# Where ACT's normalization stands in a window-attention and blur kernel, and in which step its readers run

## The chip, the cores and the metric

The program runs on one core of a Trainium2 chip. The metric is the device time of one execution in microseconds (us), lower is better. The engines are PE (TensorE), DVE (VectorE), ACT (ScalarE), POOL (GpSimd) and SP (SyncE), which here does nothing but issue DMAs. PEld are PE's weight loads.

## The reference

For each of 32 images of 192 channels and 56x56 pixels, in float32:

```python
x = x + attention(gn(x))      # gn: group norm, 32 groups
x = x + blur(gn(x))

# attention: 8x8 windows of 7x7 pixels, 12 heads of 16 channels
qkv = einsum('bchw,oc->bohw', x, w_qkv)
dots = einsum('wnid,wnjd->wnij', q, k) * scale + bias[None]
out = einsum('wnij,wnjd->wnid', softmax(dots), v)
out = einsum('bchw,oc->bohw', out, w_proj) + b_proj
# blur: channels shifted by whole pixels and filtered by 5x5 Gaussian taps
```

## The kernel before, in words

The image is the unit of an outer loop, and its 64 windows are taken as 32 pairs. One turn of `for p in range(PAIRS)` is called a **step** here; an image has steps 0 to 31, and every engine has its own written-out list of what it does in step p. `bodies` runs the image loop on each engine. Each body works on three images at once: `prev` (i-1, its second norm and blur), `att` (i, attention), `nxt` (i+1, its first norm). The order on an engine is that of the source; semaphores (`S[...]`) alone tie engines together. SP's DMAs stand in such a list too, and SP issues them strictly one after another.

What a pair p goes through:

- `scores` (PE, in step p-1), `maximum` (DVE), `turn` (PE, the transpose at L604, once a step), `shift_hi` (ACT, `mov`, L832) and `shift_lo` (DVE), `shifted` (PE, L613 and L620).
- In step p+1 `exp` (ACT, L827), `prob_hi` (DVE, L1045), `prob_lo` (POOL, L1201).
- In step p+2 `attend` (PE, L637, first thing in the step), `normalize` (DVE, `osb`). In p+3 `out_hi` (ACT, L840), `out_lo` (POOL, L1207), `turn_out` (PE, L647), `turned_out` (ACT, `om`, L848, last thing in ACT's step). `attend` of the next step waits for `turned_out`, since both share the bank `pO`.

What runs beside it, by tables of step numbers:

- `norm_step`: four steps for each chunk of two rows of windows. `norm` (ACT, L784) writes the normalized tokens twice, in float32 (`xnf`) and in float16 (`xnh`, of the last 64 channels `xnt`); `norm_lo` (POOL) and `tail_lo` (DVE, L993) form the low half from the two one step later.
- `qk_step`: query and key projections in steps 6 to 11, 14 to 19, 22 to 27 and 30 to 3 (`qk`, PE, L505 to L550 into `pQ`; `qk_hi`, ACT; `qk_lo`, DVE). The first of each four waits for all four `tail_lo` and `norm_lo` of its chunk.
- `v_step`: `values` (PE, into `pV`) in odd steps, `LEAD` = 5 pairs ahead, then `v_hi`, `v_lo`.
- `proj_step`: the output projection of window row r (`project`, PE, L658, into `pV`) in step 4r+6 (128 channels) and 4r+8 (the last 64), then `project_out` (ACT) and `add_residual` (POOL). It waits for the last `turned_out` of its row, which ACT does in that same step 4r+6.
- `blur_step`: stages of one image's blur in 16 steps each, PE's from step 13.
- SP: `stack` copies heads for `scores` (36 DMAs for each chunk), `spread_v` copies values (4 DMAs, L431), `store_x1` (L440, L442), `read_x1` (one DMA of 2.35 MB into `xr`, L448), the loads of the next image (L480, L482), the stores of the output (L492).

Of the kernel before, what the change touches and what calls it, by code (L numbers as in the profile page):

```python
# [34 lines left out]
C, HW = 192, 56  # L35
# [34 lines left out]
LEAD = 5  # L70
# [67 lines left out]
def build(nc, x, w_in, b_out, table, rel, offset, cf, ch, scratch, out):  # L138
    images = x.shape[0]
    ctx = ExitStack()  # L140
    with ctx:
# [93 lines left out]
        PER = {"x_in0": 16, "x_in": 48, "x1_out": 256, "xr_in": 16, "y_out": 8 * 16, "stack_q": 192 * NCH,  # L235
# [64 lines left out]
        def v_step(p, att, nxt):  # L300

            if p % 2 and (att if p + LEAD < PAIRS else nxt):
# [75 lines left out]
        def _(sp):  # L378
# [67 lines left out]
            def read_x1():  # L446

                sp.dma_start(xr[0:SY, :], scratch.rearrange("s y c x -> (s y) (c x)")).then_inc(S["xr_in"], 16)  # L448

            def body(i, prev, att, nxt):  # L450
                for p in range(PAIRS):
                    v = before(v_step, p, prev, att, nxt) if p % PPR == 2 else None
# [7 lines left out]
                    if p == 4 and prev:  # L460
                        store_x1(i - 1, NCH - 1)
                    if p == 5 and prev:
# [4 lines left out]
                        read_x1()  # L467
                    if p in (2, 6) and nxt:
# [12 lines left out]
                        for h in (0, 1) if p == 6 else ():  # L481
                            sp.dma_start(xt[64 * h:64 * h + 64, par(i + 1), :],  # L482
                                         xi[CM:C, h * (TOK // 2):(h + 1) * (TOK // 2)]).then_inc(S["x_in"], 16)
                    b = blur_step(p, 15, prev)
# [17 lines left out]
        def _(pe):  # L502
# [180 lines left out]

            def body(i, prev, att, nxt):
                for p in range(PAIRS):
# [7 lines left out]
                    b = blur_step(p, 13, prev)  # L693
# [15 lines left out]
                    v = v_step(p, att, nxt)  # L709
                    for n, row, tail in was:  # L710

                        if v and tail_bank(row if tail else 0) is pV:
                            pe.wait_ge(S["pj_act"], nth("pj_act", i + n, 2 * row + tail + 1))
                    if v:
# [16 lines left out]
                    if prev and p == 5:  # L731
# [4 lines left out]
                    if prev and p == 6:  # L736
                        pe.wait_ge(S["gn2_dve"], nth("gn2_dve", i - 1, 6))
                        group_sum(2, pM, gv[1]).then_inc(S["gn2_pe"], 1)
                    if prev and p == 9:
# [13 lines left out]
        def _(act):  # L753
# [6 lines left out]
            def norm(i, c, s):  # L760

                row, tail = 2 * c + s % 2, s // 2
                act.wait_ge(S["gn1_pool"], nth("gn1_pool", i, 2))

                done = PPC // 2 * (c - 1) - (0 if s % 2 else 2)
# [515 lines left out]
```

## Time and profile before

| | |
|---|---|
| Times of three executions | 6164.22, 6182.63 (median), 6187.85 us |
| The profiled execution's own time | 6163.97 us |
| Its span on the core | 6162.2 us |
| PE, DVE, ACT, POOL busy, share of the span | 88%, 69%, 62%, 58% |
| Granted clock of PE, mean share of 2.4 GHz | 0.929 |
| DMA engines busy, mean of 16 | 55% |

### The profile page before, as it was taken

What the parts mean: (1) busy time and instruction counts of PE and PEld (TensorE: products, weight loads), DVE (VectorE), ACT (ScalarE), POOL (GpSimd) and SP (SyncE); (2) the same over time, 40 slices, a digit from 0 to 9 for tenths busy, and PEclk for the clock granted to TensorE, in tenths of its full rate; (3) what the DMA queues carried; (4) which work ended last, traced back from release to release, by engine and by line L of the source; (5) the groups of instructions that cost most, each with busy time, mean ns of one, the idle gap of its engine ahead of it and who ended that gap; (6) DMA issues with size and microseconds to landing.
All of it is one profiled execution on the core that took longest, in us unless ns stands there. A gap on an engine that the chain in (4) does not pass through costs nothing. (4 is left out here: it accounts for less than half of the span.)

```text
span 6162.2 us, 258882 instructions
## 1 busy us (share of the span) xinstructions
PE 5409.0 (88%) x97992; PEld 4490.2 (73%) x97992; DVE 4255.1 (69%) x9682; ACT 3790.8 (62%) x8451; POOL 3580.1 (58%) x3940
## 2 busy tenths in 40 slices
PE   5888889988898888889888898888898889899896
PEld 3777777777777777777777777777777777777775
DVE  3776667777777767777767777767777766677763
ACT  1666666666666666666666666666666666666662
POOL 0565556665556655566655566655566655566654
PEclk9999999999999999999999999999999998999996
DMA  2555655555655555655555655555655555555553
GB/s 61 123 130 138 138 134 120 129 134 136 139 134 117 135 135 132 141 132 118 137 134 133 143 127 122 137 133 136 137 128 127 134 137 134 134 123 127 133 118 72
DMA packets 1352972, 790.32 MB, mean 128 GB/s; under 512 B 1187528, under 2 KB 1237128, under 8 KB 1344008
## 3 DMA queue, kind: packets, MB, share of 16 engines
q1 hardware_dynamic: 1351816, 774.03, 55.1%
q8 instruction: 832, 13.63, 1.0%
q14 instruction: 324, 2.65, 0.1%
HBM read 157.09 MB, written 154.14 MB: 51 GB/s over the span
## 5 line engine op out<-in xcount | busy, mean ns | idle before, releaser
L1207 POOL TENSOR_TENSOR o<-osb,o 128x192 f16<-128x192 f32 x1024 | 624.5, 610 | 1768.8 <-ACT o L840 1754.1
L1201 POOL TENSOR_TENSOR probl<-prob,probh 98x588 f16<-98x588 f32 x1024 | 1332.5, 1301 | 298.1 <-DVE probh L1045 183.8
L637 PE MATMUL pO<-vv,probh 98*49 98x34 f16 x24576 | 1023.2, 225 | 103.9 <-ACT om L848 85.6
L637 PEld LDWEIGHTS pO<-vv,probh 98*49 98x49 f16 x24576 | 872.6, 122 | 313.1 <-issue 251.7
L832 ACT ACTIVATE mov<-pT 12x98 f16<-12x98 f32 x1024 | 248.1, 242 | 1329.6 <-PE pT L604 1329.5
L637 PE MATMUL pO<-vv,probl 98*49 98x34 f16 x12288 | 995.2, 228 | 54.5 <-issue 54.5
L637 PEld LDWEIGHTS pO<-vv,probl 98*49 98x49 f16 x12288 | 778.0, 122 | 58.4 <-issue 58.3
L1030 DVE TENSOR_REDUCE mx<-pS 128x12 f32<-128x588 f32 x1024 | 777.2, 759 | 34.1 <-issue 15.9
L620 PE MATMUL pT<-qst,kst 96*98 96x49 f16 x12288 | 760.4, 208 | 11.5 <-issue 11.4
L827 ACT ACTIVATE prob<-pT 98x588 f32<-98x588 f32 x1024 | 672.3, 657 | 105.8 <-PE pT L620 97.2
L620 PEld LDWEIGHTS pT<-qst,kst 96*98 96x98 f16 x12288 | 696.5, 133 | 13.8 <-issue 13.6
L1045 DVE CAST probh<-prob 98x588 f16<-98x588 f32 x1024 | 531.4, 519 | 203.9 <-ACT prob L827 191.0
L586 PE MATMUL pS<-biasT,addb 128*64 128x294 f16 x4096 | 619.2, 312 | 18.4 <-DMA kst<-mix 17.3
L594 PEld LDWEIGHTS pS<-kst,qst 96*64 96x64 f16 x12288 | 589.2, 118 | 30.0
L594 PE MATMUL pS<-kst,qst 96*64 96x98 f16 x12288 | 610.9, 214 | 0.0
L1050 DVE RECIPROCAL rden<-pO 128x12 f32<-128x12 f32 x1024 | 233.3, 228 | 521.2 <-PE pO L637 516.4
L613 PE MATMUL pT<-mov,biasT 128*98 128x98 f16 x6144 | 479.0, 218 | 32.0 <-DVE mov L1036 29.0
L1036 DVE SCALAR_TENSOR_TENSOR mov<-pT,mov 12x98 f16<-12x98 f32 x1024 | 257.4, 251 | 354.0 <-ACT mov L832 338.7
L1004 DVE SCALAR_TENSOR_TENSOR mix<-pQ,cst,mix 128x392 f16<-128x392 f32 (+1 forms) x512 | 320.8, 627 | 242.7 <-ACT mix L810 239.0
L1231 POOL TENSOR_TENSOR xc<-xcf,xc 114x336 f16<-114x336 f32 x512 | 447.4, 874 | 69.3 <-ACT xc L891 30.2
L613 PEld LDWEIGHTS pT<-mov,biasT 128*98 128x98 f16 x6144 | 398.5, 133 | 73.4 <-ACT mov L832 45.3
L1242 POOL TENSOR_TENSOR xcf<-xr,coef 114x336 f32<-114x336 f32 x512 | 384.6, 751 | 105.7 <-DVE coef L1123 57.0
(190 smaller groups left out, 16140.3 us busy)
## 6 DMA issues: line engine op xcount, KB each, us to landing
kst<-kh SPq DMA_DIRECT2D x1536, 98.0 KB, 2.2
qst<-qh SPq DMA_DIRECT2D x1536, 49.0 KB, 2.3
qst<-mix SPq DMA_DIRECT2D x768, 98.0 KB, 2.9
kst<-mix SPq DMA_DIRECT2D x768, 98.0 KB, 2.2
vv<-cv SPq DMA_DIRECT2D x1024, 73.5 KB
xr<-x_scratch SPq DMA_DIRECT2D x32, 2352.0 KB, 12.3
out<-xr SPq DMA_DIRECT2D x256, 294.0 KB
x_scratch<-xm SPq DMA_DIRECT2D x256, 196.0 KB, 3.3
```

The costliest lines, as they stand in the source:

```text
L586: pe.matmul(pS[half, bank, 0:HB], addb[:, half], biasT[:, HB * bank:HB * bank + HB], start=True, stop=False, skip_group_check=True)
L594: mm = pe.matmul(o, qst[:, c % 2, t:t + 64], kst[:, c % 2, hp, PW * w:PW * w + PW], start=False, stop=True, skip_group_check=True)
L613: pe.matmul(pT[0:98, bank, at:at + PW], biasT[:, PW * hp:PW * hp + PW], mov[:, :], start=(hp % 3 == 0), stop=False, skip_group_check=True)
L620: mm = pe.matmul(pT[0:98, bank, a:a + NT], kst[:, c % 2, hp, PW * w:PW * w + PW], qst[:, c % 2, t:t + NT], start=False, stop=True, skip_gr ...
L637: mm = pe.matmul(pO[64 * win:64 * win + NT, OW * hp:OW * hp + OW], b[0:98, p % 2, PW * hp + NT * win:PW * hp + NT * win + NT], vv[:, g % 2 ...
L827: act.activation(banked(prob[0:98, p % 2, :]), pT[0:98, :, 0:HB], ACT.Exp).then_inc(S["exp_a"], 1)
L1030: dve.tensor_reduce(mx[:, :].rearrange("p (b h) -> p b h", b=2), src, AX.X, ALU.max).then_inc(S["max_d"], 1)
L1045: dve.tensor_copy(probh[0:98, p % 2, :], prob[0:98, p % 2, :]).then_inc(S["ph_d"], 1)
L1201: pool.tensor_tensor(probl[0:98, p % 2, :], prob[0:98, p % 2, :], probh[0:98, p % 2, :], ALU.subtract).then_inc(S["pl_p"], 1)
L1207: pool.tensor_tensor(o16[:, p % 2, C:2 * C], osb[:, p % 2, :], o16[:, p % 2, 0:C], ALU.subtract).then_inc(S["ol_p"], 1)
L1231: pool.tensor_tensor(xc[:, b % 2, 1, :], xcf[0:SX, b % 2, :], xc[:, b % 2, 0, :], ALU.subtract).then_inc(S["xcl_p"], 1)
L1242: pool.tensor_tensor(v, src, spread(coef[:, cols], HW), ALU.mult).then_inc(S["xcf_p"], 1)
```

## The change

1. `norm_step` gives every norm one step earlier (1, 9, 17, 25 in place of 2, 10, 18, 26).
2. On ACT `norm` is called twice in a step, for one output each: the float32 one ahead of `shift_hi`, with the waits, and the float16 one at the step's end, behind `turned_out`. The number of instructions stays.
3. `LEAD` is 6 and `values` run in even steps; in steps with neither `qk` nor blur they are issued ahead of `turn_out` and `shifted` on PE. Projections move to odd steps: 4r+7 and 4r+9, and 4r+8 for the tail of the last row.
4. Blur and the second norm move one step later. `read_x1` becomes two DMAs of half the size, in SP's steps 6 and 8; the second part of the next image's load moves from step 6 to 7.

```diff
-LEAD = 5
+LEAD = 6
...
-            for lo, shift, c, on in ((2, 0, 2, att), (10, 0, 3, att), (18, 1, 0, nxt), (26, 1, 1, nxt)):
+            for lo, shift, c, on in ((1, 0, 2, att), (9, 0, 3, att), (17, 1, 0, nxt), (25, 1, 1, nxt)):
...
-            if p % 2 and (att if p + LEAD < PAIRS else nxt):
+            if p % 2 == 0 and (att if p + LEAD < PAIRS else nxt):
...
-                    s = PPR * r + 6 + (LATE_TAIL if tail and r < NWX - 1 else 0)
+                    s = PPR * r + 7 + (0 if not tail else LATE_TAIL if r < NWX - 1 else 1)
...
-            def read_x1():
-
-                sp.dma_start(xr[0:SY, :], scratch.rearrange("s y c x -> (s y) (c x)")).then_inc(S["xr_in"], 16)
+            def read_x1(s):
+
+                sp.dma_start(xr[HW * s:HW * s + HW, :],
+                             scratch[s].rearrange("y c x -> y (c x)")).then_inc(S["xr_in"], 16)
...
-                    v = before(v_step, p, prev, att, nxt) if p % PPR == 2 else None
+                    v = before(v_step, p, prev, att, nxt) if p % PPR == 1 else None
...
-                    if p == 4 and prev:
+                    if p == 5 and prev:
                         store_x1(i - 1, NCH - 1)
-                    if p == 5 and prev:
+                    if p == 6 and prev:
...
-                        read_x1()
-                    if p in (2, 6) and nxt:
+                        read_x1(0)
+                    if p == 8 and prev:
+                        read_x1(1)
+                    if p in (2, 7) and nxt:
...
+                    v = v_step(p, att, nxt)
+                    early = v and not q and b is None
+                    if early:
+                        given_back(i, was)
+                        values(i + v[0], v[1])
...
-                for o in (full, hi):
-                    a = act.activation(wmajor(o), src, ACT.Identity, bias=gbias[g, tail:tail + 1],
-                                       scale=grs[0][g, tail:tail + 1])
-                a.then_inc(S["xnh_a"], 1)
+                    o = xnh[:, t] if hi else xnf[:, s % 2, :]
+                a = act.activation(wmajor(o), src, ACT.Identity, bias=gbias[g, tail:tail + 1],
+                                   scale=grs[0][g, tail:tail + 1])
+                if hi:
+                    a.then_inc(S["xnh_a"], 1)
...
+                    n, q = norm_step(p, att, nxt), qk_step(p, att, nxt)
+                    if n:
+                        norm(i + n[0], n[1], n[2], False)
                     if att:
                         shift_hi(i, p)
...
-                    n = norm_step(p, att, nxt)
-                    if n:
-                        norm(i + n[0], n[1], n[2])
-                    q = qk_step(p, att, nxt)
                     if q:
                         qk_hi(i + q[0], q[1], q[2])
-                    for n, q in at(p, 3, prev, att, nxt):
-                        turned_out(i + n, q)
+                    for m, o in at(p, 3, prev, att, nxt):
+                        turned_out(i + m, o)
+                    if n:
+                        norm(i + n[0], n[1], n[2], True)
...
-                            pool.wait_ge(S["xr_in"], nth("xr_in", i - 1, 16))
+                            pool.wait_ge(S["xr_in"], nth("xr_in", i - 1, 32))
```

ACT in the image loop, from one `mov` (`shift_hi`) to the next `prob` (`exp`), in step 2. Before:

```order
L832 ACTIVATE mov<-pT 12x98
L763 ISA
L767 REGISTER_ALU
L769 REGISTER_ALU
L774 ISA
L784 ISA
L784 ACTIVATE xnf<-xm,gbias,grs 128x392
L784 ACTIVATE xnh<-xm,gbias,grs 128x392
L789 REGISTER_ALU
L807 ACTIVATE mix<-pQ,cst 128x8x49
L810 ACTIVATE mix<-pQ,cst 64x8x49
L848 ACTIVATE om<-pO 128x3x98
```

The same place now (`xnf` ahead of `mov`, `xnh` behind `om`):

```order
L793 ACTIVATE xnf<-xm,gbias,grs 128x392
L840 REGISTER_ALU
L842 ACTIVATE mov<-pT 12x98
L799 REGISTER_ALU
L817 ACTIVATE mix<-pQ,cst 128x8x49
L820 ACTIVATE mix<-pQ,cst 64x8x49
L858 ACTIVATE om<-pO 128x3x98
L793 ACTIVATE xnh<-xm,gbias,grs 128x392
L837 ACTIVATE prob<-pT 98x588
```

The copy `om` has moved ahead of one normalization of its step, and the other now stands in front of `mov`.

SP in the image loop, from the last store of the previous image to the key stack of chunk 2. Before:

```order
L442 DMA x_scratch<-xt 32x14x56
L448 DMA xr<-x_scratch 112x5376
L425 REGISTER_ALU
L431 DMA vv<-cv 49x8x96 x4
L480 ISA
L480 DMA xm<-in_x 128x784
L482 ISA
L482 DMA xt<-in_x 64x1568
L482 ISA
L482 DMA xt<-in_x 64x1568
L407 REGISTER_ALU
L413 DMA qst<-qh 32x784 x12
```

And now:

```order
L442 DMA x_scratch<-xt 32x14x56
L448 DMA xr<-x_scratch 56x5376
L483 ISA
L483 DMA xm<-in_x 128x784
L485 ISA
L485 DMA xt<-in_x 64x1568
L485 ISA
L485 DMA xt<-in_x 64x1568
L407 REGISTER_ALU
L413 DMA qst<-qh 32x784 x12
L448 DMA xr<-x_scratch 56x5376
L425 REGISTER_ALU
```

The values' copies `vv` have moved ahead of the store, and the second half of the read stands behind the twelve `qst` copies.

## Rows read from the trace of the kernel before

**Rows 1.** The page: busy time by engine; the granted clock in 40 slices

```profile
PE 5409.0 (88%) x97992; PEld 4490.2 (73%) x97992; DVE 4255.1 (69%) x9682; ACT 3790.8 (62%) x8451; POOL 3580.1 (58%) x3940
...
PEclk9999999999999999999999999999999998999996
```

**Rows 2.** Waits of PE: who waited for whom, us, times, longest

```profile
PE pV L658 <- ACT om L848: 194.4, 125, 1.8
PE pQ L505 <- DVE xnt L993: 146.3, 128, 7.4
PE pO L637 <- ACT om L848: 85.6, 141, 1.2
PE pO L637 <- issue: 56.7, 27, 3.5
...
PE pS L586 <- DMA kst<-mix: 17.3, 11, 4.5
```

**Rows 3.** Timeline of ACT and PE, step 2 of image 12: start, duration

```profile
2361.07 0.75 ACT L784 ACTIVATE xnf<-xm,gbias,grs 128x392 f32 x1 [0.23 <-issue]
...
2361.72 0.73 ACT L784 ACTIVATE xnh<-xm,gbias,grs 128x392 f16 x1
...
2363.55 0.41 ACT L848 ACTIVATE om<-pO 128x294 f16<-128x294 f16 x1
...
2364.11 0.33 PE L658 MATMUL pV<-om,wmh 128*128 128x392 f16 x1 [1.76 <-ACT om L848]
```

**Rows 4.** Timeline of DVE and PE, step 6 of the same image

```profile
2385.17 0.55 DVE L993 TENSOR_TENSOR xnt<-xnf,xnt 64x392 f16<-64x392 f32 x1
...
2385.86 0.49 PE L505 MATMUL pQ<-xnh,wmh 128*128 128x392 f16 x1 [1.18 <-DVE xnt L993]
```

**Rows 5.** Stretches: steps 7, 16 and 5; length, engines busy, clock, DMA

```profile
2392.29:2396.64 4.35, 4.35 (x94) 3.77 (x91) 3.91 (x11) 2.38 (x6) 1.81 (x4) 1.00 1.10 297
2444.68:2449.97 5.29, 5.29 (x106) 4.32 (x102) 4.89 (x11) 3.81 (x9) 3.84 (x5) 1.00 0.27 66
2377.64:2384.41 6.77, 6.21 (x97) 5.74 (x93) 3.59 (x9) 3.43 (x7) 3.15 (x3) 0.75 0.95 287
```

**Rows 6.** Waits of ACT; then ACT's group of one normalization form

```profile
ACT mov L832 <- PE pT L604: 1329.5, 1023, 7.6
...
L784 ACT ACTIVATE xnf<-xm,gbias,grs 128x392 f32 x240 | 178.9, 745 | 7.7 <-issue 7.0
```

**Rows 7.** Timeline of PE: the first transpose of image 2 and of image 30

```profile
485.57 0.27 PE L604 MATMUL pT<-cst,mx 128*12 128x128 f32 x1
...
5700.73 0.27 PE L604 MATMUL pT<-cst,mx 128*12 128x128 f32 x1
```

**Rows 8.** Waits of SP's DMA queue

```profile
SPq L431 <- DVE cv L1022: 335.1, 110, 8.8
SPq L448 <- DMA x_scratch<-xt: 92.3, 32, 3.8
```

**Rows 9.** Timeline of SP in image 12: DMA issues, merged, duration of the issuing

```profile
2387.79 0.59 SPq L442 DMA_DIRECT2D x_scratch<-xt  x1
2391.40 0.35 SPq L448 DMA_DIRECT2D xr<-x_scratch  x1
2391.88 10.65 SPq L431 DMA_DIRECT2D vv<-cv  x4
...
2413.57 3.34 SPq L431 DMA_DIRECT2D vv<-cv  x4
...
2442.64 8.48 SPq L413 DMA_DIRECT2D qst<-qh  x12
2456.71 4.12 SPq L431 DMA_DIRECT2D vv<-cv  x4
```

**Rows 10.** DMA issues: KB each, us to landing

```profile
xr<-x_scratch SPq DMA_DIRECT2D x32, 2352.0 KB, 12.3
```

**Rows 11.** Timeline of POOL, step 10: the first use of `xr`

```profile
2411.37 0.75 POOL L1242 TENSOR_TENSOR xcf<-xr,coef 114x336 f32<-114x336 f32 x1 [1.02 <-DVE coef L1123]
```

More of the change, by code:

```diff
@@ L682, in blur, with given_back @@
                 mm.then_inc(S["c1_pe" if stage == 0 else "c2_pe"], 1)
+            def given_back(i, was):
+                for n, row, tail in was:
+                    if tail_bank(row if tail else 0) is pV:
+                        pe.wait_ge(S["pj_act"], nth("pj_act", i + n, 2 * row + tail + 1))
             def body(i, prev, att, nxt):
@@ L692, in body @@
                         turn(i, p)
-                    b = blur_step(p, 13, prev)
+                    b = blur_step(p, 14, prev)
                     if b is not None:
@@ L708, in body @@
                         blur(i - 1, b, 1)
[L709 to L714, printed above, removed]
+                    if v and not early:
+                        given_back(i, was)
                         values(i + v[0], v[1])
@@ L758, in _, with norm @@
             act.wait_ge(S["setup"], SET_ALL)
-            def norm(i, c, s):
+            def norm(i, c, s, hi):
                 row, tail = 2 * c + s % 2, s // 2
-                act.wait_ge(S["gn1_pool"], nth("gn1_pool", i, 2))
-                done = PPC // 2 * (c - 1) - (0 if s % 2 else 2)
-                if due("v_pe", i, done):
-                    act.wait_ge(S["v_pe"], nth("v_pe", i, done))
-                if due("qk_pe", i, 6 * (c - 1)):
-                    act.wait_ge(S["qk_pe"], nth("qk_pe", i, 6 * (c - 1)))
-                if tail:
-                    act.wait_ge(S["xnl_p"], nth("xnl_p", i, 2 * c + s - 1))
-                elif due("xtl_d", i, 2 * c + s - 1):
-                    act.wait_ge(S["xtl_d"], nth("xtl_d", i, 2 * c + s - 1))
+                if not hi:
+                    act.wait_ge(S["gn1_pool"], nth("gn1_pool", i, 2))
+                    done = PPC // 2 * (c - 1) - (0 if s % 2 else 2)
+                    if due("v_pe", i, done):
+                        act.wait_ge(S["v_pe"], nth("v_pe", i, done))
+                    if due("qk_pe", i, 6 * (c - 1)):
+                        act.wait_ge(S["qk_pe"], nth("qk_pe", i, 6 * (c - 1)))
+                    if tail:
+                        act.wait_ge(S["xnl_p"], nth("xnl_p", i, 2 * c + s - 1))
+                    elif due("xtl_d", i, 2 * c + s - 1):
+                        act.wait_ge(S["xtl_d"], nth("xtl_d", i, 2 * c + s - 1))
                 t = slice(ROW * (row % 4), ROW * (row % 4) + ROW)
@@ L1092, in body @@
                         maximum(i, p)
-                    if prev and p == 5:
+                    if prev and p == 6:
                         aggregate(1, i - 1)
@@ L1140, in body @@
                                      ).then_inc(S["gn2_bn"], 1)
-                    for n, t, on in ((0, 0, att and p == 26), (0, 1, att and p == 30), (-1, 2, prev and p == 2),
-                                     (-1, 3, prev and p == 4)):
+                    for n, t, on in ((0, 0, att and p == 27), (0, 1, att and p == 31), (-1, 2, prev and p == 3),
+                                     (-1, 3, prev and p == 5)):
                         if on:
```

41 lines of the change are left out of this document (20 added, 21 removed).

## The prediction

> **What bounds the kernel now.** Read first the busy shares and the granted clock [rows 1]: PE is busy 88% of the span and nothing else is over 69%, and the clock falls a little in most slices. So PE is the engine whose gaps cost time. Next the waits of PE [rows 2]. Three of them are large, and all three lead to ACT's step: the projection waits for `om` (194.4 us), the query projection for `xnt` (146.3), `attend` for `om` (85.6). Together 426.3 us, over 32 images 13.3 us an image. Then the timeline of one such place [rows 3]: in step 2 ACT does both normalizations (0.75 and 0.73 us) and a key copy before `om`, which starts at 2363.55; PE starts projecting at 2364.11 after 1.76 us of nothing. Step 6 shows the other kind [rows 4]: the last `xnt` is written in the step in which PE needs it, 1.18 us idle.
>
> Then ask which other resource is close behind. SP has no busy share, so take its waits [rows 8]: 335.1 us for the values' low halves and 92.3 us for its own stores, 427.4 us in all, 13.4 us an image. All other time it issues. An image takes (5700.73 - 485.57) / 28 = 186.3 us [rows 7], so SP works 186.3 - 13.4 = 172.9 us of it. That twelve copies cost it 8.48 us, 0.71 each, is seen in [rows 9]. PE already waits 11 times for a stack that SP brought late (17.3 us [rows 2]). SP is the second limit, and a near one.
>
> PE alone would allow much less: a step with a query and a value projection and no wait takes 4.35 us, one with blur 5.29 [rows 5]. Sixteen of each are 154 us; with the group sums and the steps that lack filler I put PE's own floor at 160.
>
> **Part by part.**
>
> *Norm one step earlier.* The last `tail_lo` of a chunk falls in step 5, 13, 21, 29, the query projection that needs it in 6, 14, 22, 30. `tail_lo` takes 0.55 us [rows 4], so a whole step of slack covers it: the 146.3 us go (4.6 an image). What ACT's norm waits for (the readers of the buffer it overwrites) lies further back, since `values` are also one step earlier.
>
> *Projections one step later.* In 4r+7 the row's last `om` is a step old. The 194.4 us go (6.1 an image). The residual and the second norm's statistics come later with them, which is why blur moves by a step too: its distance to them shrinks for the last row alone, whose tail is now two steps later while blur is one.
>
> *Norm in two parts.* The number of instructions stays, so this adds nothing to ACT's busy time. The first part (0.745 us [rows 6]) stands ahead of `mov`, where ACT waits 1329.5 us in 1023 cases, 1.30 us on average [rows 6]; that idle time hides it. `om` comes earlier by both parts in its step, so `attend` need not wait for it: 85.6 us go (2.7 an image). The second part stands ahead of `exp`; `exp` feeds DVE and POOL and is needed by `attend` two steps on, more than a step of slack. If the cover in front of `mov` is gone, `mov` is late, and with it PE's `shifted`: step 16, with keys and blur and without norm, has ACT busy 3.81 us of 5.29 [rows 5]; with the two parts (0.75 + 0.73 [rows 3]) that is 5.29, just PE's time. Six steps an image are so full. I charge nothing for them beside SP, and at most 0.3 us each, which is in the range.
>
> *Values in even steps, and early where PE has no filler.* The same matmuls. The order on SP changes: `spread_v` is a step earlier, so SP finds its data sooner. I price it with SP.
>
> *The read in two halves.* The whole read (2.35 MB, 12.3 us to landing [rows 10]) blocks SP: the four value copies behind it take 10.65 us where others take 3.34 [rows 9], 7.3 us too many. Halves of about 6 us, with other issues between them, should block less. It can go from 0 (the same bytes, and the loads of the next image now stand right behind the first half) to all 7.3. I take a third, 2.3 us, nearer to the lower end, because the bytes are the same. PE's own "issue" wait of 56.7 us [rows 2] lies in the window of that read; I credit nothing, because PE is no longer the limit.
>
> **The sum.** PE's side gives 186.3 - 13.3 = 173.0 at today's clock. SP's side gives 172.9 of work, plus 2.9 for its own stores (92.3 / 32; nothing stands between the stores and the read, so it stays), minus 2.3 of blocking, plus what is left of the waits for values. These are 10.5 an image now (335.1 / 32), between 0 and 10.5 after. I take 1.5, near zero, because a PE that runs 6% faster asks SP for the same copies in less time, so SP is late more often than early. 172.9 + 2.9 - 2.3 + 1.5 = 175.0 us. The two sides are close; SP's is the larger one, and the time follows it. Saved are 11.3 us in each of 31 images (the first has no blur beside it): 350 us. The profiled execution took 6163.97 us, its span being 6162.2, so 5814. It is the fastest of those shown; scaled to their median (6182.63 / 6163.97 = 1.003) this is 5831, and I say 5830.
>
> The clock: step 5 runs at 0.75 and takes 6.77 us [rows 5], and the mean is 0.929. Fewer PE waits should raise it, but where SP sets the pace a faster PE only waits longer, so it has no term of its own.
>
> What the Trainium skill says of SP's cost ("DMA: Bandwidth & Descriptors", section "Issuing engines are not separate DMA queues") is that the sequencer's time to start a DMA is usually small against the DMA itself. By that rule SP would not bind and the rival next would hold. The trace disagrees: SP works 172.9 of 186.3 us.
>
> **The rivals.**
>
> *PE follows freely (deeper gain).* The read's blocking goes whole and SP never waits but for its stores: 172.9 + 2.9 - 7.3 = 168.5, and PE is below that with its waits, its 56.7 us of issue and part of the clock back. 17.8 x 31 = 552 us, 5612, scaled 5630. For it: PE's floor of 160. Against: SP's blocking depends on bytes, and two limits this close rarely leave no wait.
>
> *Half of it comes back.* The second half of the read stands behind twelve `qst` copies. From the read's issue to its first use there were 2411.37 - 2391.40 = 20.0 us [rows 9, 11]; one step later and with shorter steps some 22. Now the second half is issued up to 7 (blocked loads) + 8.5 us after the first and lands 6 later: 22, or more where SP is late already. POOL stands at L1242 until then, with the low halves of norm and probabilities behind it, for which ACT's next norm and `attend` wait. 5 us an image are 155 us: 5985. Part of it would be covered by SP's own lateness in these steps, which is why it is not my forecast.
> On the same read the Trainium skill ("DMA: Bandwidth & Descriptors", "Why a DMA increments its semaphore by 16 and not by 1") has an HWDGE copy use as many engines, up to 16, as divide both outer sizes: 16 for 112 rows, 14 for 56. An estimate from that page: 14% longer halves, a microsecond more of lateness. No row here shows a read of 56 rows.
>
> *Slower: both parts of norm exposed.* Should ACT reach `mov` without idle time in the norm steps, the first part delays `mov` and the second delays `exp`, and PE pays 0.75 + 0.73 us in 16 steps: 23.7 us an image against 13.3 won, 10.4 x 31 = 322 us more, 6486, scaled 6505. It decides where ACT's idle time ahead of `mov` is under 0.75 us in those steps. For it: they are ACT's fullest. Against: the mean of 1.30 us [rows 6], and that `om`, which stood behind 1.5 us of norm, now frees PE earlier.
>
> *Only the names change.* PE's waits turn to `mov`, `osb` and stacks, and the total stays: 6180. It would need SP or ACT to be the limit already, against SP's 13.4 us of waits.
>
> **How the numbers follow.** Forecast 0.50, deeper gain 0.15, half comes back 0.23, names only 0.05, slower 0.07. The forecast's own range is 5730 to 5900 (the blocking from 0 to all, leftover waits from 0 to 4). To hold 8 in 10, the range reaches into both neighbours: 5670 to 6010. A change under 0.5% is one that timing this kernel can't tell from none. Faster 0.88, within 0.5% 0.05, slower 0.07.
>
> **What would show it.** In the profile after, `PE <- ACT om` of the projection and `PE pQ <- DVE xnt` should be nearly gone, and `attend`'s wait for `om` below a third. SP's waits for values should fall from 335 to under 100 us, while PE waits for `DMA kst<-mix` or other stacks for 50 to 200 us: that is the sign of SP as the limit. The copies behind each half of the read should take under 8 us. `mov`'s idle time should fall by some 0.4 us on average, not to zero. I am wrong if SP still waits 250 us or more (then ACT or PE holds the pace), if POOL waits for `DMA xr` by more than 100 us (the half that comes back), or if PE's waits for `DVE mov` exceed 150 us (the slower case).

## The result, and the profile after

| | before | after |
|---|---|---|
| Median | 6182.55 us | 5950.59 us (four executions, 5941.65 to 5956.22) |
| Ratio after / before | | 0.9629, 95% interval [0.9605, 0.9652] |
| Span of the profiled execution | 6162.2 us | 5954.4 us |
| Granted clock, mean | 0.929 | 0.927 |
| PE, DVE, ACT, POOL busy | 88%, 69%, 62%, 58% | 90%, 72%, 64%, 60% |

The change makes the kernel 3.7% faster. The forecast was 5830 us, 5.7% faster; the time came out 121 us above it, inside the range of 5670 to 6010 but outside the forecast's own 5730 to 5900. Lines below are those of the kernel after: `shift_hi` is now L842, `turned_out` L858, the query projection L508 (it shares that helper line with `values` and the blur's matmuls), `attend` L640, `scores` L589 and L597.

The transposes that open image 2 and image 30, in PE's timeline, which answer to [rows 7]:

```profile
472.63 0.27 PE L607 MATMUL pT<-cst,mx 128*12 128x128 f32 x1
...
5498.43 0.27 PE L607 MATMUL pT<-cst,mx 128*12 128x128 f32 x1
```

An image takes (5498.43 - 472.63) / 28 = 179.5 us, 6.8 less than before (186.3). The forecast had 175.0.

Next the waits, which answer to [rows 2, 6, 8]: who waited for whom, us in total, times, longest.

```profile
ACT mov L842 <- PE pT L607: 997.7, 717, 7.9
...
POOL xcf L1253 <- DMA xr<-x_scratch: 105.9, 32, 13.3
...
PE pS L589 <- issue: 96.8, 30, 4.0
...
PE pS L589 <- DMA kst<-mix: 87.4, 38, 5.2
...
PE pM L508 <- DVE z L1143: 83.7, 136, 1.1
...
PE pM L508 <- DVE xr L1123: 68.6, 135, 0.9
...
PE pQ L508 <- DVE xnt L1004: 9.9, 2, 7.4
```

Neither wait for `om` is left among PE's larger ones (2.1 us together), and of the 128 waits for `xnt` two remain, one of them at the start. So 414 of the 426.3 us named in the prediction went. But the waits of PE in this view, all added up, fell only from 731 to 576 us. Five others grew: for instructions (`issue`, all lines) from 68 to 137; for the stack `kst` from 17.3 to 87.4; for DVE's `z` from 44.0 to 83.7 and for its `xr` from 10.4 to 68.6; and for DVE's `mx` from 0.7 to 30.9. That is 69 + 70 + 40 + 58 + 30 = 267 given back.

SP's waits after:

```profile
SPq L448 <- DMA x_scratch<-xt: 107.3, 32, 4.1
SPq L413 <- DVE qh L1015: 91.3, 49, 30.0
SPq L440 <- POOL xt L1207: 79.6, 31, 16.5
...
SPq L431 <- DVE cv L1033: 15.6, 18, 6.3
```

The wait for values fell from 335.1 to 15.6. SP still works 171.8 us an image (179.5 less its gaps, which in its timeline sum to 7.7 an image over images 2 to 29), against 172.4 by the same reading of before (to about 0.5 us, by which short gaps are counted). For 96% of an image it has a DMA to issue.

That this is now on the critical path, the page of the kernel after shows in the chain of work that ended last:

```profile
SPq 40%; PE 34%; issue 9%; ACT 6%; DVE 6%; DMA 4%; POOL 0%; ACTq 0%; DVEq 0%; POOLq 0%
```

The chain itself, in order of time (start, length, what), where it leaves SP in step 6 of image 12 and where it comes back to SP in step 23:

```profile
2300.99 2.83 DMA kst<-mix
2304.05 0.46 PE pS L589 x2
...
2405.28 0.57 DVE qh L1015
2405.87 1.99 SPq L413
```

Over images 2 to 29 SP's issues are 77.6 us of the chain in an image, 66.7 of them between step 23 and step 6 of the next image. In the page of before the chain is followed for 1% of the span only, so it can't be compared.

SP's timeline from the read to the third value copy of image 12, which answers to [rows 9] (start, duration of the issuing):

```profile
2311.93 0.37 SPq L448 DMA_DIRECT2D xr<-x_scratch  x1
2312.53 0.39 SPq L483 DMA_DIRECT2D xm<-in_x  x1
2313.17 1.39 SPq L485 DMA_DIRECT2D xt<-in_x  x2
2314.81 8.09 SPq L413 DMA_DIRECT2D qst<-qh  x12
2322.94 0.57 SPq L448 DMA_DIRECT2D xr<-x_scratch  x1
2323.64 12.11 SPq L431 DMA_DIRECT2D vv<-cv  x4
...
2353.24 3.41 SPq L431 DMA_DIRECT2D vv<-cv  x4
```

The first half blocks nothing that can be seen: twelve `qst` copies behind it take 8.09 us, as elsewhere. The second half, of half the bytes, holds the four `vv` copies for 12.11 us, longer than the whole read did (10.65): the first two take 0.91 and 0.82 us, the other two 4.96 and 5.29. What the value copies behind a read take beyond their usual 0.81 us each is called the hold-up below. By SP's timeline of images 2 to 29 it is 7.8 us an image before and 8.0 after. POOL at that time:

```profile
2335.80 0.75 POOL L1253 TENSOR_TENSOR xcf<-xr,coef 114x336 f32<-114x336 f32 x1 [3.29 <-DMA xr<-x_scratch]
```

The second half is issued at 2322.94 and used at 2335.80: 12.9 us for 1.18 MB, where the whole 2.35 MB took 12.3 to land [rows 10]. The trace's packets of 21.5 KB took 1.65 us each in the first half (median of the images' means), against 1.29 in the whole read of before. PE, meanwhile, lacks instructions:

```profile
2324.23 0.46 PE L589 MATMUL pS<-biasT,addb 128*64 128x294 f16 x2 [3.13 <-issue]
...
2336.10 0.25 PE L616 MATMUL pT<-mov,biasT 128*98 128x98 f16 x2 [2.01 <-issue]
```

Both lie near the second half: the first gap, from 2321.10, begins before its issue, the second ends as it lands. Stretches of image 12 (length; PE, PEld, DVE, ACT and POOL busy; clock; DMA share; GB/s) for steps 6, 9, 13 and 16, against [rows 5]:

```profile
2295.95:2305.17 9.22, 7.46 (x102) 6.18 (x98) 4.37 (x12) 2.40 (x6) 3.15 (x3) 0.70 0.77 204
...
2316.81:2324.86 8.05, 4.92 (x89) 3.61 (x86) 4.98 (x15) 4.38 (x9) 4.82 (x6) 0.91 0.91 198
2344.65:2352.39 7.74, 6.75 (x92) 5.41 (x88) 4.76 (x13) 2.52 (x6) 4.82 (x5) 0.67 0.61 144
2363.77:2369.06 5.29, 5.29 (x112) 4.72 (x108) 3.97 (x10) 4.35 (x10) 4.12 (x6) 1.00 0.27 65
```

Step 16 has no gap: 5.29 us is PE's own time. The image's loss is in a few steps: 6 (a stack 1.75 us late, then half clock), 9 (instructions), 13 (half clock for part of it). Summed over the means of images 2 to 29, steps 0 to 7 went from 46.2 to 43.9 us, 8 to 13 from 37.6 to 38.4, 14 to 21 from 46.6 to 45.1, 22 to 31 from 55.9 to 52.2.

The third price, DVE's, in step 19 (DVE's timeline, then PE's wait):

```profile
2378.94 1.13 DVE L1056 CAST probh<-prob 98x588 f16<-98x588 f32 x1 [0.48 <-ACT prob L837]
2380.10 0.51 DVE L1123 SCALAR_TENSOR_TENSOR xr<-pM,xr 112x336 f32<-112x336 f32 x1
...
2380.75 0.23 PE L508 MATMUL pM<-amat,xc 114*112 114x112 f16 x1 [0.85 <-DVE xr L1123]
```

DVE waits 0.48 us for ACT's `prob` (ACT now does `xnh` ahead of it), and the blur's `xr`, behind `probh` in DVE's order, frees PE's bank 0.85 us late. 135 such cases make the 68.6 us.

### The profile page after: what moved, and what is told of

Same layout as the page of the kernel before. It is cut to its first block, busy times and chain, and to the rows that moved or that the text cites. A ratio compares the mean times of both kernels' runs of the same rounds, so it can differ in the third digit from the quotient of the medians.

```text
span 5954.4 us, 258943 instructions
## 1 busy us (share of the span) xinstructions
PE 5360.8 (90%) x97992; PEld 4454.5 (75%) x97992; DVE 4277.5 (72%) x9682; ACT 3801.5 (64%) x8451; POOL 3569.0 (60%) x3940
## 3 DMA queue, kind: packets, MB, share of 16 engines
q8 instruction: 832, 13.63, 1.0%
## 4 chain that ended last, share of the span: by engine, by line
SPq 40%; PE 34%; issue 9%; ACT 6%; DVE 6%; DMA 4%; POOL 0%; ACTq 0%; DVEq 0%; POOLq 0%
SPq L413 16%; SPq L419 13%; SPq L431 6%; PE pO L640 6%; PE pT L623 3%; PE pS L589 2%; PE pS L597 2%; PE pM L508 2%; PE pT L616 2%; SPq L495 2%; DMA xr<-x_scratch 2%; DMA kst<-mix 1%; PE pT L607 1%; PE pM L510 1%; PE pM L509 1%
## 5 line engine op out<-in xcount | busy, mean ns | idle before, releaser
L1218 POOL TENSOR_TENSOR o<-osb,o 128x192 f16<-128x192 f32 x1024 | 607.5, 593 | 1449.0 <-ACT o L850 1430.8
L640 PE MATMUL pO<-vv,probh 98*49 98x34 f16 x24576 | 1018.2, 225 | 7.4 <-issue 6.0
L640 PEld LDWEIGHTS pO<-vv,probh 98*49 98x49 f16 x24576 | 866.5, 121 | 211.3 <-issue 156.4
L640 PE MATMUL pO<-vv,probl 98*49 98x34 f16 x12288 | 990.2, 228 | 0.0
L842 ACT ACTIVATE mov<-pT 12x98 f16<-12x98 f32 x1024 | 245.1, 239 | 999.1 <-PE pT L607 997.7
L589 PE MATMUL pS<-biasT,addb 128*64 128x294 f16 x4096 | 613.4, 310 | 215.3 <-issue 96.8
L640 PEld LDWEIGHTS pO<-vv,probl 98*49 98x49 f16 x12288 | 765.4, 121 | 0.0
L1056 DVE CAST probh<-prob 98x588 f16<-98x588 f32 x1024 | 544.9, 532 | 160.5 <-ACT prob L837 133.6
L597 PE MATMUL pS<-kst,qst 96*64 96x98 f16 x12288 | 603.6, 212 | 1.2 <-issue 1.2
L597 PEld LDWEIGHTS pS<-kst,qst 96*64 96x64 f16 x12288 | 580.1, 117 | 31.1 <-issue 1.4
L1253 POOL TENSOR_TENSOR xcf<-xr,coef 114x336 f32<-114x336 f32 x512 | 388.9, 760 | 143.5 <-DMA xr<-x_scratch 105.9
L858 ACT ACTIVATE om<-pO 128x294 f16<-128x294 f16 x1024 | 424.4, 414 | 55.5 <-PE pO L650 46.1
```

The lines of the kernel that those rows point to most:

```text
L589: pe.matmul(pS[half, bank, 0:HB], addb[:, half], biasT[:, HB * bank:HB * bank + HB], start=True, stop=False, skip_group_check=True)
L597: mm = pe.matmul(o, qst[:, c % 2, t:t + 64], kst[:, c % 2, hp, PW * w:PW * w + PW], start=False, stop=True, skip_group_check=True)
L640: mm = pe.matmul(pO[64 * win:64 * win + NT, OW * hp:OW * hp + OW], b[0:98, p % 2, PW * hp + NT * win:PW * hp + NT * win + NT], vv[:, g % 2 ...
L1056: dve.tensor_copy(probh[0:98, p % 2, :], prob[0:98, p % 2, :]).then_inc(S["ph_d"], 1)
L1218: pool.tensor_tensor(o16[:, p % 2, C:2 * C], osb[:, p % 2, :], o16[:, p % 2, 0:C], ALU.subtract).then_inc(S["ol_p"], 1)
```

## The experiments

All ratios are to the kernel before (medians 6175 to 6186 us), with a 95% interval. The kernel after stands at 0.9629. Image times in this section come from the first transposes of images 2 and 30, as above.

**One read again,** whole, in step 6.

```diff
-                        read_x1(0)
-                    if p == 8 and prev:
-                        read_x1(1)
+                        read_x1()          # 112 rows at once, in step 6
```

> The kernel after, with the read of x1 as one DMA of 112 rows in SP's step 6 again; all else as after. Theory Q (SP's queue sets the pace and the second half of the read, which lands 12.9 us after its issue and blocks four value copies for 12.1 us, is where gain was lost): POOL's wait for xr (105.9 us) falls under 30, the blocked copies take 10 to 11 us, and the time falls to 5800 to 5900 us. Theory P (PE's own chains through DVE and ACT set the pace; SP's lateness is hidden): within 0.5% of after's 5950. A third: the whole read blocks what stands behind it more than two halves do, as the change assumed: 5960 to 6010.

Measured: 5970.96 us, 0.969 [0.9665, 0.9714], 0.6% of the time before above the kernel after; the third theory had it. So the halves are worth a little, and the whole read has a price of its own:

```profile
DVE gst L1164 <- DMA xt<-in_x: 146.8, 31, 11.0
...
PE pS L586 <- DVE mx L1038: 84.1, 66, 9.4
```

POOL's wait for the read is down to its one case in the first image. In its place the loads of the next image, which now stand behind the whole read, land late; DVE stands at their statistics (for `xt` 146.8 us, against 41.7 with the halves), and `maximum` behind them holds PE, up to 9.4 us at a time. The halves traded one late transfer for another. The hold-up fell from 8.0 to 4.9 us an image and PE's wait for instructions (all lines) from 137 to 80 us, and neither made the kernel faster.

**The same halves cut by columns.** Both halves of 112 rows, at the same places.

```diff
-                sp.dma_start(xr[HW * s:HW * s + HW, :],
-                             scratch[s].rearrange("y c x -> y (c x)")).then_inc(S["xr_in"], 16)
+                t = slice(CC * HW // 2 * s, CC * HW // 2 * (s + 1))
+                sp.dma_start(xr[0:SY, t], scratch.rearrange("s y c x -> (s y) (c x)")[:, t]).then_inc(S["xr_in"], 16)
```

> The kernel after, with the read still in two DMAs at the same two places, each of all 112 rows and half the columns in place of 56 rows and all columns. If the shape of a half (56 rows, packets of 21.5 KB at 1.65 us) is what made the second half slow: each half is done in 4 to 5 us in place of 7, and the time is 5820 to 5900. If it is the place of the second half behind the twelve qst copies: 5930 to 5960, with POOL's wait for xr still above 80 us.

Measured: 5866.96 us, 0.9511 [0.949, 0.9532], 1.2% of the time before less. SP behind the second half:

```profile
2302.14 0.58 SPq L449 DMA_DIRECT2D xr<-x_scratch  x1
2302.84 7.38 SPq L431 DMA_DIRECT2D vv<-cv  x4
```

The same bytes, at the same place, block 7.38 us instead of 12.11; the hold-up is 3.5 us an image instead of 8.0. POOL's wait for the read falls from 105.9 to 31.1, PE's for instructions at `scores` from 96.8 to 61.8. So the shape of a half has a price of its own: 56 rows in packets of 21.5 KB (1.65 us each) against 112 rows in packets of 10.75 KB (0.63 us each). The edit changes rows and packet size together; that the whole read, of 112 rows in packets of 21.5 KB, has a smaller hold-up than two halves (4.9 against 8.0 us) speaks for the rows. The Trainium skill ("DMA: Bandwidth & Descriptors", "Why a DMA increments its semaphore by 16 and not by 1") would have 14 engines for 56 rows and 16 for 112. The direction agrees, but the 14% estimated from that page are far less than 12.11 against 7.38.

**Half of the value copies left out, in the kernel after and in the kernel before.**

```diff
-                for w in (0, 1):
+                for w in (0,):
```

> The kernel after with two of the four value copies of each spread_v left out (w = 1 is not copied, so half of attention's values are the start's zeros): 16 of SP's some 200 issues an image, 13 to 14 us of SP's work. Theory Q: the image falls by 7 to 12 us, the time to 5600 to 5740 us. Theory P: SP just waits longer, 5900 to 5950.

> The kernel before with the same value copies left out. Theory Q: before, SP waited 10.5 us an image for values and was not the limit, so the time falls by 0 to 1.3% (6100 to 6182 us), much less than the same edit takes from after. Theory P: the same small fall in both. If SP had been the limit before the change too: below 6000.

Measured: after, 5783.94 us, 0.9383 [0.9361, 0.9405]; before, 6137.39 us, 0.9945 [0.9925, 0.9966]. The same relief of SP is worth 2.5% (0.9629 - 0.9383) in the one and 0.55% in the other, where SP's wait for values merely doubles:

```profile
SPq L431 <- DVE cv L1022: 685.7, 173, 9.8
```

In the kernel after, the wait for the stack goes from 87.4 to

```profile
PE pS L589 <- DMA kst<-mix: 7.7, 3, 4.4
```

This shows the turn that the prediction rests on: SP was not the limit before, and is a limit after. But SP then works only 154.3 us an image, 17.5 less, and the image falls by 5.6 us (to 173.9). SP's share of the chain falls from 40% to 2%: after 5.6 us the next limit takes over. The time lies between the two theories (5600 to 5740, 5900 to 5950), which had SP set the pace wholly or not at all. It limits a part of the image. The hold-up by the read is not gone with the value copies: it moves to the `kst` copies behind them (7.4 us an image over their usual time, against 1.5).

**The halves alone, in the kernel before.** The edit of the change to `read_x1` and its places (steps 5 and 8), nothing else.

> The kernel before with the read of x1 in two halves of 56 rows, the second behind the twelve qst copies of step 8, and nothing else changed. If halves by rows are slow by their shape (7 us each in place of 8.5 for the whole): POOL waits for xr by 60 us or more and the time is 6190 to 6280 us. If the split by itself is a gain: 6100 to 6170.

Measured: 6366.97 us, 1.0309 [1.028, 1.0338]: slower by 3.1%, and above the 6280 us that was expected at most. Here the rival "half of it comes back" is pure. POOL and PE in image 12:

```profile
2496.34 0.75 POOL L1245 TENSOR_TENSOR xcf<-xr,coef 114x336 f32<-114x336 f32 x1 [18.69 <-DMA xr<-x_scratch]
```

```profile
2497.86 0.48 PE L650 MATMUL pO<-identh,o 128*128 128x128 f16 x3 [9.13 <-POOL o L1210]
```

POOL stands 18.7 us at the read, `out_lo` behind it is late, and PE loses 9.1 us. Summed, POOL waits 385.1 us and PE 184.6 for `o`; the time rose by 189 (6366.97 - 6177.69). In the kernel after, blur is a step later and the second half, still in step 8, has a step more; the same cut costs it 105.9 us of POOL and hardly any wait of PE for `o` (3.3 us).

**The normalization in two parts alone, in the kernel before.** The edits to `norm` and to ACT's body, with the old tables.

> The kernel before with norm in two parts at the two places of ACT's step, all step tables as before. The projection's wait for om (194.4 us) should fall under 60 and attend's (85.6) under 40, that of the query projection for xnt stay at some 146. Theory P (PE's waits are the time): 5930 to 6000 us. Theory Q (SP follows with little to spare): 6000 to 6080, with part of the gain turned into waits for stacks.

Measured: 6127.89 us, 0.9918 [0.9887, 0.9949]. PE's waits:

```profile
PE pQ L505 <- DVE xnt L995: 141.4, 128, 7.4
PE pS L586 <- DMA kst<-mix: 85.4, 38, 4.2
PE pO L647 <- DVE osb L1057: 77.8, 81, 1.7
PE pV L658 <- ACT om L849: 76.9, 127, 0.9
```

`attend`'s wait for `om` (85.6) is gone and the projection's fell from 194.4 to 76.9: 203 us won. Back came 68 of the stack, 41 of `osb` and 28 of the blur's `xr`, and the mean clock was 0.915, against 0.929: PE was busy for 5462 us, against 5409, with the same instructions. The time moved by 50, less than either theory had (6080 at most).

**The change with the normalization undivided** (both parts at the old place, the tables of the change):

```diff
-                    if n:
-                        norm(i + n[0], n[1], n[2], False)
...
+                    if n:
+                        norm(i + n[0], n[1], n[2], False)
+                        norm(i + n[0], n[1], n[2], True)
                     for m, o in at(p, 3, prev, att, nxt):
```

> The kernel after with norm undivided, both outputs one after the other ahead of the query copies as in the kernel before, all step tables as after. If the tables carry the gain, as I think: 5950 to 6040 us, with attend's wait for om between 80 and 250 us. If the division carries it: above 6080.

Measured: 5981.78 us, 0.9683 [0.9654, 0.9711]. With the new tables the division is worth 0.5%, though PE's waits show 208.8 us for it:

```profile
PE pO L640 <- ACT om L858: 208.8, 326, 1.7
...
PE pS L589 <- DMA kst<-mix: 26.5, 16, 5.1
```

It takes away 208.8 us of waiting for `om`, and the stack's wait goes from 26.5 to 87.4, that for DVE's `xr` from 10.4 to 68.6. When the first wait in a step goes, the next resource fills the gap. The clock takes its part too: with the division all of PE's waits together fall from 645 to 576 us, but PE's busy time rises from 5304 to 5361, the mean clock being 0.927 against 0.946 (0.943 to 0.946 in the four executions without the division, 0.927 to 0.934 in the four with it). So of 70 us less waiting 57 went to a slower clock.

**Norm one step earlier alone, in the kernel before.**

```diff
-            for lo, shift, c, on in ((2, 0, 2, att), (10, 0, 3, att), (18, 1, 0, nxt), (26, 1, 1, nxt)):
+            for lo, shift, c, on in ((1, 0, 2, att), (9, 0, 3, att), (17, 1, 0, nxt), (25, 1, 1, nxt)):
```

> The kernel before with norm_step alone changed to 1, 9, 17, 25; everything else as before, norm undivided. PE's wait for xnt (146.3 us) should fall under 20. The projections in 4r+6 then wait for om in steps 2, 10, 18 as before (norm runs in 1 to 4). Theory P: the time falls by all of it and some clock, 5960 to 6040. Theory Q: a part only, since SP's copies for steps 7 and 31 are close behind, 6040 to 6120, with more than 60 us of new PE waits for DMA.

Measured: 6201.92 us, 1.0034 [1.0013, 1.0055]. Of the 146.3 us for `xnt` 7.5 are left, and nothing is won, against both theories:

```profile
PE pV L658 <- ACT om L848: 184.9, 126, 1.6
PE pO L637 <- ACT om L848: 144.8, 237, 1.2
PE pM L505 <- DVE z L1132: 83.1, 115, 1.1
```

`attend`'s wait for `om` grew by 59 us, `z`'s by 39, the stack's by 24, `mx`'s by 35, that for the value stack `vv` by 5: 162 in all. That norm meets other work of DVE and ACT in steps 1, 9, 17 and 25 is the likely reason; it was not tested. By itself this edit is no gain; together with the division it is.

**The read on ACT's queue.** Halves by columns, issued by ACT at the ends of its steps 8 and 9; SP neither issues the read nor waits for its stores ahead of it.

```diff
+                    if p == 8 and prev:
+                        act.wait_ge(S["x1_out"], nth("x1_out", i, 0))
+                        ...
+                        read_x1(0)
+                    if p == 9 and prev:
+                        read_x1(1)
```

> The kernel after with the read in two halves by columns (112 rows each), issued from ACT's own DMA queue at the end of its steps 8 and 9, POOL waiting for each half only where its columns begin (blur block 0 and 8); SP no longer waits for its stores nor stands behind the read. Theory Q: SP loses 3.4 us of waiting and 8 us of blocking an image, time 5680 to 5800 us. Theory P: as the variant with halves by columns on SP's queue, 5850 to 5890.

Measured: 5858.78 us, 0.9482 [0.9455, 0.951], against 0.9511 with the columns on SP: intervals that overlap. SP is relieved of its wait of 107 us, but not of the hold-up. Its value copies after ACT's read, in image 12:

```profile
2295.01 9.58 SPq L431 DMA_DIRECT2D vv<-cv  x4
```

The hold-up is 5.9 us an image, where it was 3.5 with the columns on SP: it follows the read, whichever engine issues it. So most of the 3.1 us an image that SP no longer waits for its stores is lost to it again. PE's wait for the stack stays at 90.7 us, and SP's share of the chain is 35% in both kernels, all but 0.7 and 1.5 us an image of it from step 23 to step 6. So with columns SP's limit no longer lies in steps 7 to 10, where the read is, but in the stretch that ends at step 6.

**A sixteenth of the read,** of all rows; the kernel leaves out the rest of the blur's input:

```diff
+                t = slice(0, CC * HW // 16)
...
-                        read_x1(0)
-                    if p == 8 and prev:
-                        read_x1(1)
+                        read_x1()
```

> The kernel after with only the first sixteenth of x1's columns read back, in one DMA of 112 rows in step 6 (the other columns of xr keep what they held, so most of the blur's input is left out); 147 KB in place of 2352 KB. If the bytes of the read are what makes PE's instructions come late (PE pS <- issue, 96.8 us in after) and blocks SP: that wait falls under 20 us, the value copies behind it take 3.4 us, and the time is 5650 to 5780. If PE's issue wait comes from elsewhere (its code, other copies): it stays at 60 us or more, and the time is 5800 to 5870, as with halves by columns.

Measured: 5783.46 us, 0.9339 [0.9312, 0.9366], at the upper end of the first theory (5780).

```profile
PE pS L587 <- DMA kst<-mix: 106.0, 33, 5.4
...
PE pS L587 <- issue: 3.3, 6, 1.2
```

The instruction wait goes from 61.8 (columns) and 96.8 (rows) to 3.3. PE's wait for instructions in steps 9 to 11 thus depends on the bytes of the read. Steps 9, 10 and 11 take 4.6, 5.7 and 4.6 us on average, 6.5 less than the 21.5 of the kernel after; steps 12 and 13 give 1.3 of it back, step 13 at a mean clock of 0.51. The stack's wait, in step 6 and before the read, does not profit, as it should not.

**The output stores on ACT's queue too.** Edit to the kernel with the read on ACT: SP's `out` stores (two in each of four steps) are ACT's, in steps 21, 24, 29 and 31.

```diff
+                    b = {21: 3, 24: 7, 29: 11, 31: 15}.get(p) if prev else None
+                    if b is not None:
+                        act.wait_ge(S["y_dve"], nth("y_dve", i - 1, b + 1))
+                        ...
+                            act.dma_start(v[h][:, c], src[:, c]).then_inc(S["y_out"], 16)
```

> The kernel with the reads on ACT's queue, and now the eight stores of the output too, at the ends of ACT's steps 21, 24, 29 and 31: SP has some 7 us less to issue an image, most of it ahead of the copies that scores of step 6 waits for. Theory Q: PE's wait for DMA kst<-mix (90.7 us) falls under 30, and the time to 5700 to 5800 us. Theory P: within 0.5% of the variant without (5859).

Measured: 5770.17 us, 0.9329 [0.93, 0.9357], another 1.5%. The wait for the stack falls from 90.7 to 13.5 us (in step 6 it is 0.07 us an image), and step 6 takes 6.6 us, where it took 9.4. In image 12 of the kernel before this edit the four pairs of stores took SP 1.14, 1.28, 1.20 and 2.67 us, in steps 19, 23, 27 and 31. The last two, 3.9 us, stand in the stretch from step 23 to step 6 in which SP was the chain. The image falls by 3.7 us (176.9 to 173.2), and SP's share of the chain from 35% to 5%.

**The read in four parts by columns,** in ACT's steps 8, 10, 12 and 13; POOL waits for the part it needs.

```diff
-                t = slice(CC * HW // 2 * s, CC * HW // 2 * (s + 1))
+                t = slice(CC * HW // 4 * s, CC * HW // 4 * (s + 1))
...
-                    if p == 9 and prev:
-                        read_x1(1)
+                    if p in (10, 12, 13) and prev:
+                        read_x1({10: 1, 12: 2, 13: 3}[p])
...
-                        if b == NB // 2:
+                        if b and b % (NB // 4) == 0:
```

> The kernel with columns, ACT's queue for the read and ACT's queue for the output stores (0.9329 of the kernel before; steps 9 to 11 of an image wait for PE's instructions, PE pS <- issue 57.8 us), and in it the read in four parts by columns, 0.59 MB each, issued in ACT's steps 8, 10, 12 and 13, where the two halves of 1.18 MB stood in steps 8 and 9. POOL needs them in steps 11, 15, 19 and 23. Theory A (the instruction wait comes from long transfers at one stretch that fill the DMA engines; with a sixteenth of the columns it had gone): parts of half the size with pauses between them let the instruction transfers through; PE pS <- issue falls under 20 us, steps 9 to 11 get shorter by 3 us an image together, and the time is 1 to 1.5% under the one with halves: ratio 0.920 to 0.925. Rival B (the bytes in these steps count, not how they are cut): issue stays at 50 to 60 us, only it is spread over steps 9 to 14; ratio 0.931 to 0.935. Rival C (the clock takes it back): issue goes but steps 12 and 13 run at half clock, as in the run with a sixteenth of the columns; ratio 0.928 to 0.933.

Measured: 5706.39 us, 0.9232 [0.9206, 0.9259], the fastest of all and 4.1% under the kernel after. PE is busy 93% of the span, and its waits are:

```profile
PE pM L491 <- DVE z L1145: 83.4, 136, 1.1
PE pM L491 <- DVE xr L1125: 68.4, 135, 0.9
PE pO L633 <- DVE osb L1068: 42.4, 61, 0.9
...
PE pS L572 <- issue: 20.4, 17, 2.3
```

The same bytes, cut finer and set apart, take the instruction wait from 57.8 to 20.4 us. Steps 9 to 11 shrink from 17.8 to 15.4 us an image. Theory A expected under 20 us and 3 us; it holds, with both numbers just short. An image takes 171.0 us. The hold-up of SP's copies goes too, from 5.4 to 0.5 us an image, but SP was hardly in the chain any more, and the steps that got shorter are those of the instruction wait. What is left is DVE's order in steps 19 to 21 and 27 to 29 (the first two rows, the same in all experiments on the kernel after but the one without the division), and step 13, which still runs at half clock:

```profile
2248.43:2256.22 7.79, 7.45 (x89) 6.09 (x87) 4.76 (x13) 2.51 (x6) 4.79 (x5) 0.50 1.00 233
```

## Why the prediction came out as it did

**PE's three waits: right, with their mechanism.** 414 of the 426.3 us went: `xnt` by the earlier norm (it goes with that edit alone), `attend`'s `om` by the division (208.8 us come back without it), and the projection's `om` by its later step, since it stays away when the division is undone. But no edit brings what it removes: the division alone 50 us of 203, the earlier norm alone nothing of 146.

**SP as the second limit: right in kind, wrong in extent.** SP's wait for values fell to 15.6 (forecast: under 100), PE's for the stack rose to 87.4 (forecast: 50 to 200), and leaving out value copies is worth over four times as much after as before. But the forecast let SP set the pace of all 32 steps. In the chain SP has 40%. It sets the pace from step 23 to the stacks of step 6 of the next image, and in the kernel after, in part of the images, once more behind the read (9 us an image in steps 7 to 14, which are gone from the chain with columns). Elsewhere PE, ACT and DVE set it. The edits agree: taking two pairs of stores, 3.9 us, out of that stretch shortened the image by 3.7; taking the wait for its stores, just behind that stretch, off SP brought nothing that stands clear of noise; and with half of the values SP's work fell by 17.5 us an image and the image by 5.6, until the next limit.

**The term that was mis-sized: blocking by the read.** The prediction took 2.3 us an image off SP's 172.9, between 0 and 7.3. Measured: the hold-up was 7.8 us an image before and is 8.0 after, so nothing was saved, and SP's work fell from 172.4 to 171.8. The copies behind each half were to take under 8 us; behind the first nothing is held up (8.09 us for twelve, the usual price), behind the second four took 12.11. A half of 56 rows isn't half a read. With columns the copies take 7.38, the hold-up is 3.5, 4.3 less than before, and SP works 166.9 us an image, 5.5 less: the cut by rows lies at the lower end of the bounds, the cut by columns past their middle. The second term, 1.5 us of SP's other waits, came to 7.7 - 107.3 / 32 = 4.3. By the forecast's own sum, measured: 171.8 of work + 3.4 for the stores + 4.3 = 179.5. Of the 4.5 us missed, 1.2 are blocking not saved, 0.5 the wait for the stores and 2.8 SP's other waits. These are mostly not for values: 91.3 us for DVE's `qh` (30.0 of it at the start) and 79.6 for POOL's `xt`: SP waits where the other engines set the pace. The base of the sum was a little off as well: it took all of SP's time outside two waits for work, where other short waits (`SPq L419 <- DVE mix`, 21.3 us) make it 172.4 and not 172.9.

**The rival "half of it comes back" happened in part.** POOL waited 105.9 us for the read, over the 100 named as its sign. The sum it gave was 5985, nearer to the time (5951) than the forecast's 5830. The two sides of the truth are both visible: SP's limit from the forecast, the late half from the rival. But that POOL's wait is what cost the time is not shown: with the whole read it was down to 10.4 us, and the kernel was slower. The chances, 0.50 and 0.23, favoured the forecast too much: it counted on the same edit for a saving that the rival counted as a loss, and the trace of before had no row for it.

**The range: partly luck.** It held 5951 because it had been widened toward the rival. The forecast's own 5730 to 5900 did not hold it, and did not follow from its terms either: with no blocking saved and 4 us of waits left, the sum is 172.9 + 2.9 + 4 = 179.8, which is 5980 us, not 5900; at the other end PE's side of 173.0 gives 5770. Measured were just these upper bounds, nothing saved and 4.3 left.

**Not in any case: PE's instructions.** "I credit nothing" for PE's issue wait was the other error. It doubled, from 68 to 137 us, a rise as large as that of the wait for the stack (70). With the whole read in the kernel after it is 80, so 57 of the rise go with the halves by rows. The row was there [rows 2], a wait for issue within the window of the read, but it would not have given the size: the same halves in the kernel before let it fall to 37, while PE stood at `o` for 184.6.

**Not in any case: DVE.** The prediction saw six full steps on ACT and charged nothing for them, with 0.3 us each in the range. They reached PE by way of DVE: PE's wait for `xr` rose by 58 us, and falls back to 10.4 without the division; that for `z` rose by 40, and did so with the earlier norm alone. Together 98 us, 3.1 us an image. What is now lost to `xr` and `z` lies in steps 19 to 21 and 27 to 29.

**`mov`: right.** ACT's wait ahead of it fell from 1.30 us on average to 997.7 / 1024 = 0.97, by 0.33 (forecast 0.4), and PE waits for `mov` 28 us, not 150. The slower case did not come near.

**Clock: the mean stayed, 0.929 and 0.927, but its parts did not.** The clock was 0.915 with the division alone and 0.946 with the tables alone. The tables' gain and the division's loss cancel, which the prediction had not weighed.

## What to carry to other kernels

Price the removal of a wait by what the next resource allows in the same steps, not by the wait's size and not by that resource's sum over the whole loop. A large read in a loop costs in three places at once, the issuer behind it, its consumer, and the instruction supply of the engines; here it paid to cut it so that each part keeps all its rows, and to set the parts apart. Giving the read to another engine's queue did not lift the hold-up. When an issuer is nearly full, look in the chain for the stretch in which it sets the pace, and take something out there: eight stores moved to another queue, two pairs of them in that stretch, were worth 1.5%.

## What the runs showed of the hardware

- Half the rows are not half a transfer: 1.18 MB in 56 rows held the copies behind it for 12.11 us, and the same bytes in 112 rows (and smaller packets) for 7.38. The hold-up was 8.0 us an image for two halves of 56 rows, 4.9 for one read of all 2.35 MB in step 6, 3.5 for two halves of 112 rows, and 0.5 for quarters set apart.
- The hold-up is not a matter of one issuer's queue: with the read issued by ACT, four of SP's value copies took 9.58 us, where 3.4 is usual, and the hold-up was 5.9 us an image. It does not fall on the first copy behind the read: behind the second half the first two took 0.91 and 0.82 us, the next two 4.96 and 5.29, and with only two value copies it moved to the `kst` copies after them. Why it begins there the runs do not show.
- PE can lack instructions because of data transfers. Instructions come as packets over the same DMA engines (832 packets, 13.63 MB in an execution, by the page's line on the queue "instruction"), and PE's wait for them at `scores` was 96.8 us with halves by rows, 61.8 by columns, 20.4 with quarters set apart, 3.3 with a sixteenth of the bytes. The 16 KB instruction packets themselves take as long in all these kernels (median 1.12 to 1.14 us). That the packets queue behind the read's is the likeliest mechanism; the runs show the dependence, not the queueing itself. The dependence has exceptions: in the kernel before, all waits for instructions fell from 68 to 37 us with halves by rows.
- Step 13 ran at a mean clock of 0.5 to 0.7 in 16 of the images 2 to 29 in the kernel after and in 16 to 27 in those made from it, against 1 in the kernel before, and stayed there when the waits ahead of it got smaller. In the kernel with quarters the only waits of PE in steps 12 and 13 of image 12 are 0.73 and 0.34 us for `osb`. Why the clock falls just there stays open; it was not tried to fill those gaps.
